# Linear attention and expert-choice MLP on one core: the folded sums are masked one step earlier on VectorE, and phi's low half goes ahead of the power on GpSimd

## The reference

```python
xn = _layernorm(x)                                  # no scale, no shift
Q = elu(xn @ Wq.T + bq) + 1;  K = elu(xn @ Wk.T + bk) + 1;  V = xn @ Wv.T + bv    # 16 heads of 16
KV = einsum('bshd,bshe->bhde', K, V);  K_sum = K.sum(axis=1)
Z = 1.0 / (einsum('bshd,bhd->bsh', Q, K_sum) + 1e-06)
attn = einsum('bshd,bhde,bsh->bshe', Q, KV, Z).reshape(b, s, E) @ Wo.T + bo
# experts choose tokens: 8 experts, each takes the best 256 tokens of a sequence
probs = softmax(xn @ gate_w);  g, m = top_k(transpose(probs), 256)
h = gelu(xn[m] @ w1) @ w2
ffn = zeros.at[m].add(g * h).astype(bfloat16)
out = x + attn + ffn
```

## Time and profile before

| | us |
|---|---|
| median of 3 runs | 1935.5 |
| lowest, highest | 1933.32, 1935.91 |
| the profiled execution | 1936.62 |
| its span | 1934.9 |

### The profile page before, as it was taken

How to read it: one execution, slowest core, us unless ns; L and a number is a source line. 1 busy time by engine, 2 the same in 40 slices (tenths; PEclk the granted TensorE clock), 3 DMA queues, 4 the chain that set the end, 5 groups by cost and what they waited for, 6 DMA issues and landing times. The chain is left out here.

```text
span 1934.9 us, 39920 instructions
## 1 busy us (share of the span) xinstructions
PE 1853.7 (96%) x13916; PEld 1297.6 (67%) x13916; DVE 1317.7 (68%) x2665; ACT 1262.7 (65%) x2030; POOL 1072.7 (55%) x981
## 2 busy tenths in 40 slices
PE   5899989899989999999999999999999999999998
PEld 3576767667776666666666666666666666666666
DVE  6678888888876777755678876555555555555556
ACT  5887877666736666666666666666666666666664
POOL 6567667666644555554555555455455455455453
PEclk9999999989999999999999999999999999999999
DMA  7778787988946655666667676676666667676667
GB/s 189 204 199 260 180 245 210 229 206 213 249 129 164 139 122 120 136 167 162 164 141 182 156 183 154 159 174 148 173 157 176 157 151 185 149 184 159 172 128 218
DMA packets 449188, 338.27 MB, mean 175 GB/s; under 512 B 225043, under 2 KB 430614, under 8 KB 449046
## 3 DMA queue, kind: packets, MB, share of 16 engines
q1 hardware_dynamic: 383958, 253.84, 47.7%
q0 software_dynamic: 48864, 66.88, 19.0%
q10 hardware_dynamic: 16224, 15.73, 2.5%
HBM read 185.61 MB, written 100.40 MB: 148 GB/s over the span
## 5 line engine op out<-in xcount | busy, mean ns | idle before, releaser
L2002 PE MATMUL pY<-w2s,hid 128*128 128x256 f16 x6144 | 756.7, 273 | 1.9 <-DVE hid L1847 1.8
L1987 PE MATMUL pH<-xgT,w1s 128*128 128x512 f16 (+1 forms) x3120 | 747.7, 376 | 1.3 <-PEq L329 1.3
L2002 PEld LDWEIGHTS pY<-w2s,hid 128*128 128x128 f16 x6144 | 599.8, 98 | 181.8 <-DVE yo L1863 3.9
L1761 POOL DMA_INDIRECT acc<-yo,idx x254 | 406.5, 1600 | 516.0 <-DVE yo L1863 443.0
L1847 DVE SCALAR_TENSOR_TENSOR hid<-gel,cur,hid 128x512 f16<-128x512 f32 (+1 forms) x520 | 384.5, 740 | 448.4 <-ACT hid L1786 349.5
L1783 ACT ACTIVATE gel<-pH,cur 128x512 f32<-128x512 f32 (+1 forms) x520 | 353.9, 680 | 482.7 <-PE pH L1987 411.5
L1987 PEld LDWEIGHTS pH<-xgT,w1s 128*128 128x128 f16 x3120 | 305.2, 98 | 252.3 <-DMA xgT<-xg 1.6
L1786 ACT ACTIVATE hid<-gel,cur 128x512 f16<-128x512 f32 (+1 forms) x520 | 372.0, 715 | 17.1
L224 POOL DMA_INDIRECT xg<-table,idx x256 | 292.8, 1144 | 111.9 <-issue 59.0
L742 POOL TENSOR_TENSOR phk<-phik,phk 128x256 f16<-128x256 f32 x128 | 93.5, 731 | 169.4 <-ACT phk L832 169.3
L1863 DVE TENSOR_SCALAR yo<-pY,gains,cur 128x256 f32<-128x256 f32 x256 | 121.6, 537 | 13.8 <-PE pY L2002 12.3
(11 more groups left out here) (248 smaller groups left out, 2046.4 us busy)
## 6 DMA issues: line engine op xcount, KB each, us to landing
stage<-in_w SPq DMA_DIRECT2D x160, 512.0 KB, 5.0
xring<-in_x SPq DMA_DIRECT2D x16, 1024.0 KB, 6.5
x2ring<-in_x SPq DMA_DIRECT2D x16, 1024.0 KB, 6.8
table<-xhl SPq DMA_DIRECT2D x32, 512.0 KB, 4.1
mix<-x2ring SPq DMA_DIRECT2D x32, 512.0 KB
acc<-zeros SPq DMA_DIRECT2D x16, 1024.0 KB, 5.4
fmix<-mix SPq DMA_DIRECT2D x48, 256.0 KB
facc<-acc SPq DMA_DIRECT2D x48, 256.0 KB
```

The lines of the kernel that those rows point to most:

```text
L1761: g.indirect_dma_start(acc, bass.IndirectOffsetOnAxis(ap=idx[q][:, s:s + 1], axis=0), yo[i][:, s, :], None, compute_op=ALU.add).then_inc(a ...
L1987: last = t.matmul(pH[hc % 4][:, tok], w[:, aw, c, hc * P:(hc + 1) * P], xgT[i][:, ad, c, tok], start=k == 0 and c == 0, stop=k == 2 and c ...
L2002: last = t.matmul(pY[s // 2][:, s % 2, :], hid[:, hc % 4, ad, s * P:(s + 1) * P], w[:, aw, hc, :], start=hc == 0 and k == 0 and s % 2 == 0 ...
```

## The change

Three pieces of program order are changed; no instruction is added, removed or altered. On VectorE `blocks_out(m)` goes from step 2 (behind `split_rest`) to step 1, behind `low(n, 5)` and ahead of `gate_probs(n - 1, 1)`. On GpSimd `norm` is split into the addition of epsilon (`norm`) and the power (`root`); in step 3 the order becomes `norm(n + 1)`, `key_low(n, 2)`, `root(n + 1)`, `centre(n + 1, 0)`, and in step 4 `key_low(n, 3)`, `centre(n + 1, 1)`. In steps 5 to 7 the order stays.

```diff
@@ GpSimd: norm, split
                     g.tensor_scalar(veps[:, :], moments[:, :, 1], 1e-5, None, ALU.add).then_inc(veps_done, 1)
+
+                def root(n):
                     pool.wait_ge(veps_done, at(veps_done, n))
                     pool.wait_ge(rstd_done, at(rstd_done, n, -1))
                     g.tensor_tensor(rpow[:, :], veps[:, :], minus_half[:, :], ALU.pow).then_inc(rpow_done, 1)
@@
                 norm(0)
+                root(0)
@@ GpSimd: the body
                         if nxt and j == HALF - 1:
                             norm(n + 1)
-                        if nxt and j >= HALF - 1:
+                        if nxt and j > HALF:
                             centre(n + 1, j - (HALF - 1))
                         if j > 0:
                             key_low(n, j - 1)
                         elif n > 0:
                             key_low(n - 1, NT - 1)
+                        if nxt and j == HALF - 1:
+                            root(n + 1)
+                        if nxt and j in (HALF - 1, HALF):
+                            centre(n + 1, j - (HALF - 1))
@@ VectorE: the body
                             if j == 2:
                                 split_rest(m)
-                                blocks_out(m)
@@
                             low(n + 1, j - HALF - 1)
+                        if s2 and j == 1:
+                            blocks_out(m)
                         if j == 1 and n > 0:
                             gate_probs(n - 1, 1)
```

## The result

The changed kernel takes 1902.4 us (median of four runs, 1902.07 to 1902.76) against 1934.4 us for the kernel before in the same comparison. The ratio is 0.9836, with a 95% interval from 0.9819 to 0.9854: 32 us faster. The forecast was 1907 us, in a range from 1894 to 1926.

What follows compares the result with a forecast made beforehand. TensorE, busy 96% of the span, was taken as the bound, losing time to waits for kvT and phk and clock falls. Batches 2 to 15 going from 471.6 to 442.6 us saved 29 us: 1907 us, range 1894 to 1926.

Steps and rivals of the forecast that it cites:

- The gap for kvT, and the margin: TensorE before fold_o in batch 13: the 2.36 us gap goes with the mask in step 1, margin 0.7 us.
- The other end of the bound: VectorE work behind the mask starts 0.35 us later; in batch 3 k_feature(n, 1) is late by up to 1.3 us.
- What is late next: TensorE at q_part(n, 1): waits for ScalarE's qraw, so 1.25 of the 2.36 us come back.
- GpSimd's order: key_low(n, 2) ahead of power and centring: TensorE's stall before sum_kv(n, 2) is 0.2 us instead of 1.84 in batch 3.
- VectorE's q_feature behind the power: q_feature(n, 1) waits for GpSimd's power to end: gain there 1.5 us blocked, 2.05 us not.
- The clock: TensorE's clock stays up, since the remaining gap is shorter than every one that a fall followed.
- rival 1: The clock still falls behind the new gaps in most of thirteen batches: 19 us, 1926 us; chance 0.18.
- The price of a fall: One fall of TensorE's clock costs 0.05 x 33.6 = 1.7 us in a batch.
- The stretch and what lies around it: Batches 2 to 15 take 442.6 us against 471.6; batches 0 and 1 counted 0, the second stage untouched.
- rival 2: q_feature gets in ahead of the power (5 us) and k_feature(n, 1) comes earlier (7 us): 1895 us; chance 0.14.
- Rival 3: k_feature(n, 1) pushed under GpSimd's addition everywhere by 1.3 us: 1933 to 1936 us, no change; chance 0.05.
- Rival 4: Later power and centring make rstd and batch n + 1's centred tiles the bound, past 3 us cover: 1950 us; chance 0.06.

Runs made afterwards that it cites:

- e4: Changed kernel with the mask at the head of step 2, ahead of split_rest, instead of in step 1; 1916.5 us, ratio 0.9919.
- e3: Changed kernel with ScalarE's sums_out(n - 1) moved ahead of key_high(n, 1) in step 2; 1899.5 us, ratio 0.9832.
- e7: On e3, the top-k slots of steps 1 and 2 moved behind q_feature in step 3; 1908.2 us, ratio 0.9871.
- e1: The VectorE edit alone: mask in step 1, GpSimd in the order of the kernel before; 1949.1 us, ratio 1.0085.
- e2: The GpSimd edit alone: changed kernel with the mask back in step 2; 1924.7 us, ratio 0.9952.
- e5: On e4, GpSimd's second addition of bo left out, so bo is missing in tiles 2 and 3 of most batches; 1903.2 us, ratio 0.9850.
- e9: On e3, GpSimd's four additions of bo in steps 2, 5, 6 and 7 instead of 1, 2, 5 and 6; 1895.9 us, ratio 0.9792.

## Why the prediction was right or wrong

**The gap for kvT, and the margin.** Right. `fold_o` runs without a gap, `kvT` done 0.5 us ahead of it. The shift of 0.35 us of what is queued behind was absorbed where the prediction said: in batch 7 the probabilities took 0.51 instead of 0.83 us and ended together with the addition of bo, and `k_feature(n, 1)` started 7.2 us after the denominators in both kernels. The other end of the bound came true too, in batches 3 to 5: there the probabilities fell under the addition and took 1.13 us instead of 0.23. Batch 3 took 30.08 us, against 29.20 in e4, without the mask in step 1, and 29.19 in e3, where `sums_out` doesn't stand behind `key_high(n, 1)`. VectorE in batch 3 of the changed kernel:

```profile
112.87 1.13 DVE L1060 TENSOR_TENSOR probs<-gexp,grec 128x32 f32<-128x32 f32 x1
```

**What is late next.** The engine was right, the wait was not. The prediction went from `fold_o` to `q_part(n, 1)` and read `qraw` as the next wait, 1.25 us. It passed over `sum_kv(n, 0)` between the two, which waits for `sums_out(n - 1)`, a step earlier in ScalarE's same queue. TensorE stands there for 1.65 us, and after it `qraw` (done at 240.56) is no wait at all for a `q_part` at 240.90. e3 shows both: without the first wait the second appears, with 0.62 us. That the sum didn't suffer is no merit of this step: the output hangs on ScalarE's queue and not on this gap, and e3 gained 0.19 us a batch by taking it away.

**GpSimd's order.** Right, with its number: `sum_kv(n, 2)` was to start 462.15 - 448.74 = 13.4 us after the denominators and started after 13.36.

**VectorE's q_feature behind the power.** Wrong. The prediction took the blocked value, because the power would lie over it in full. In the trace after, `q_feature` started at 244.64 in the middle of the power (243.66 to 245.31) and took 0.69 us, its usual length. The output came 17.9 us after the denominators; the forecast had 18.7 blocked, 18.1 unblocked. This is the term that was mis-sized: 0.8 us in nine batches, 7 us. 0.55 of it is the block that didn't come, the rest the way to `q_feature`, which started 14.25 us after the denominators where the walk had 14.5 unblocked. It brought 32.2 us a batch where 31.4 were measured.

**The clock.** Right, with luck. It stayed up in all fourteen batches, and rival 1 didn't happen. But the reason given, that the gap is shorter than every one that a fall followed, doesn't hold as a rule: the clock fell in batch 11 of e7 behind a gap of 1.43 us, less than the 1.65 here, and it stayed up in batch 8 of e1 behind 2.92 us. The price of a fall, 1.7 us, was right (1.68 in e2). Batch 11 of e7:

```profile
376.42 3.38 PE L1417 MATMUL pO<-mo,qz 128*128 128x256 f32 x8 [1.43 <-issue]
...
356.68:391.64 34.96, 31.58 (x288) 23.76 (x287) 32.20 (x89) 22.66 (x49) 21.43 (x24) 0.95 0.77 212
```

**The stretch and what lies around it.** What TensorE needs by itself, 29.1 us in the prediction, was right: batch 3 took 29.19 us in e3. 442.6 us were forecast for the fourteen batches and 435.1 measured, 7.5 us too careful. In batches 2 to 5 122.8 stood against 122.6, but batch 4 was 0.7 us too long in the forecast and batch 5 0.8 too short, which is luck. Batches 0 and 1 were costed at nothing and lost 2.1 us. In batch 0 TensorE stood 2.52 us for a transpose:

```profile
33.23 0.41 PE L1328 MATMUL pP<-wkg,xT 128*128 128x272 f16 x2 [2.52 <-DMA xT<-xhl]
```

In the kernel before the same projection started at 31.86 without a wait. But e1, which runs these batches in the order of the kernel before, has that wait too, with 1.66 us, and lost nothing by it: its denominators of batch 2 came at 73.80. The eleven traces with the new order on GpSimd have them between 75.81 and 77.49. So the loss goes with GpSimd's order, and by which wait is open.

**The rivals.** Half of rival 2 came true, and not by its way: `q_feature` didn't get in ahead of the power, it ran beside it unhindered, and that is most of the distance from 1907 to 1902. Its other half, an earlier `k_feature(n, 1)`, didn't come. Rival 3, with `k_feature(n, 1)` pushed under the addition everywhere, happened in batches 3 to 5 alone. e1 shows that the mask alone is worth less than nothing, it loses 15 us, but by the clock and not by rival 3's way. The prediction summed the two edits along one walk, which is why its total held; it said nothing that would have let a reader foresee that one edit without the other is slower. Rival 4 has no trace at `keys(n, 5)`, which had its cover, but the later power does bind in e3 and e4, through `rstd` in VectorE's queue. The price of the contention that the prediction weighed, from nothing to 1.3 us for a shift of 0.35, was found in e4 in another place, on `split_rest` (1.36 us on `sum_kv(n, 2)`).

The page "SBUF — State Buffer" of the Trainium skill, section "Who interferes with whom", says that a VectorE instruction with two SBUF inputs contends with a GpSimd instruction that reads SBUF, and calls the shared port pair an exclusive lock. That fits the addition of bo and `key_low` in e4, e5 and e7. It doesn't fit the power on 8 columns as applied in the prediction's sum: the `q_feature` that started 0.98 us into it wasn't held, nor was one that started 0.24 us into it (e3, e9). With 0.16 us between the starts (e4) it was the power that took 0.70 us longer. Which part of the power reads SBUF isn't shown here.

## What to carry to other kernels

When a wait is removed, walk the waiting engine's own program from that point instruction by instruction and list every wait in the text, bank releases too; the view of waits names only the last event, which here was an unrelated instruction of another engine. Two edits in series on the bound engine need not add up: alone they were worth -15 and +9 us, together 32. Taking away the first wait alone made the second longer, and moved the fall of the clock to where nothing covered it. A gap on the bound engine isn't a gain by its length either: one of 1.65 us was worth 0.19, since another engine's queue ran beside it. Before VectorE's order is changed by a few tenths of a microsecond, lay its two-input instructions beside GpSimd's long ones: which pair overlaps decided 13 us here.

## What the runs showed of the hardware

A VectorE instruction of 0.29 us on SBUF operands took 1.25 us when it started 0.15 us behind GpSimd's addition of two tiles (1.26 us, e4); a cast took 0.72 beside a `key_low` of 0.67 us; `low` took 1.49 against 0.45 (e7). A `q_feature` of 128x512 with both inputs in SBUF wasn't held by a power on 128x8 that ran from 1.0 us ahead of it to the end (0.69 us, after). The power took 1.66 us there and with `q_feature` 0.24 us behind its start (e3, e9), and 2.36 us with `q_feature` 0.16 us behind its start (e4). Of two batches with the same gap of 2.36 us one was followed by a fall of the clock and one was not (e2). A fall followed a gap of 1.43 us in e7 and none a gap of 2.92 us in batch 8 of e1. An uncovered fall cost 1.68 us in e2 and 1.61 in e1.
